# Attention and feed-forward kernel: the residual's mean and variance in the epilogue from sums that ScalarE accumulates, in place of VectorE's statistics

## The reference, cut to what matters

```
def _layernorm(x, axis=-1, eps=1e-05):
    m = jnp.mean(x, axis=axis, keepdims=True)
    v = jnp.var(x, axis=axis, keepdims=True)
    return (x - m) / jnp.sqrt(v + eps)
...
def _L0_ffn_ref(inputs, ln_w, ln_b, W1, b1, W2, b2):
    x = bf16_round(inputs)
    residual = bf16_round(inputs)
    h = mx_layernorm(x, ln_w, ln_b)      # mean and variance of the bf16 residual
    h = mx_linear(h, W1, b1)             # mx_quant of h and W1, 512 -> 2048
    h = mx_gelu(h)
    h = mx_linear(h, W2, b2)             # 2048 -> 512
    return bf16_round(residual + h)
...
    x = x + _L0_xattn_ref(_layernorm(x), ctx_2048, ...)
    x = x + _L0_ffn_ref(_layernorm(x), ...)
```

## Time and profile before

| | |
|---|---|
| median of 3 runs | 2685.33 us (2680.43 to 2685.69) |
| profiled execution: time | 2687.95 us |
| profiled execution: span | 2686.2 us |
| granted TensorE clock, mean | 0.844 |
| busy: VectorE, TensorE, ScalarE, GpSimd | 92%, 82%, 75%, 54% |

### The profile page before, as it was taken

One profiled execution on the slowest core, in us unless ns is written; L12 is line 12 of the kernel. 1 busy time (PEld: TensorE's weight loads), 2 busy tenths in 40 slices (PEclk: granted clock), 3 DMA queues, 4 the chain that ended last, 5 costly groups with the idle time before them and its releaser, 6 DMA issues. The chain is left out here.

```text
span 2686.2 us, 53043 instructions
## 1 busy us (share of the span) xinstructions
PE 2212.1 (82%) x20020; PEld 1181.0 (44%) x20020; DVE 2478.9 (92%) x3614; ACT 2009.7 (75%) x1862; POOL 1443.9 (54%) x1879
## 2 busy tenths in 40 slices
PE   8999999788887787777888888787787777868886
PEld 4454445344444444444444444444444444433433
DVE  6998758699999999999999999999999999957997
ACT  4454444389888888888888888888888888855655
POOL 2432322155767666676666667676666767551001
PEclk9999999877778877887677777878878888779999
DMA  7566454699999999999999999999999999990000
GB/s 234 145 154 143 97 135 101 150 184 182 193 193 203 202 179 201 199 189 184 191 205 173 205 201 186 191 198 203 178 199 202 183 199 177 175 226 19 16 20 24
DMA packets 1406612, 445.65 MB, mean 166 GB/s; under 512 B 1337444, under 2 KB 1377892, under 8 KB 1405256
## 3 DMA queue, kind: packets, MB, share of 16 engines
q1 hardware_dynamic: 1391816, 403.47, 80.4%
q10 hardware_dynamic: 14624, 40.06, 5.9%
HBM read 80.66 MB, written 44.02 MB: 46 GB/s over the span
## 5 line engine op out<-in xcount | busy, mean ns | idle before, releaser
L913 DVE TENSOR_SCALAR_CACHE_REDUCE arena<-a_ps_s 128x1281 f32<-128x1281 f32 (+1 forms) x1280 | 1824.3, 1488 | 23.7 <-PE a_ps_s L853 16.6
L960 ACT ACTIVATE arena<-arena,a_bias,a_row_scale 128x3328 uint8<-128x3328 f32 (+1 forms) x512 | 1560.5, 3049 | 241.9 <-POOL a_bias L1019 241.3
L853 PE MATMUL a_ps_s<-arena,q_rep 96*128 96x512 bf16 (+2 forms) x3840 | 1201.6, 434 | 345.6 <-DVE arena L913 313.9
L853 PEld LDWEIGHTS a_ps_s<-arena,q_rep 96*128 (+1 forms) x3840 | 310.7, 108 | 782.8 <-DVE arena L913 456.5
L866 PEld LDWEIGHTS a_ps_o<-v_head,a_nT 128*128 128x128 f16 x13056 | 524.3, 102 | 263.6 <-issue 148.5
L866 PE MATMUL a_ps_o<-v_head,a_nT 128*128 128x32 f16 x13056 | 514.1, 182 | 28.9 <-POOL a_nT L1027 26.2
L1026 POOL CAST a_nT<-arena 128x1664 int16<-128x1664 uint8 x256 | 401.8, 1569 | 211.1 <-DMA arena<-arena 205.7
L1027 POOL CAST a_nT<-arena 128x1664 int16<-128x1664 uint8 x256 | 402.8, 1573 | 0.0
L1015 POOL TENSOR_SCALAR a_row_max<-a_row_max,a_part_max 128x1 f32<-128x1 f32 x256 | 92.1, 360 | 348.4 <-DVE arena L913 339.8
L376 POOL TENSOR_TENSOR p_rest<-p_kq,p_parts 128x512 f32<-128x512 f32 (+1 forms) x51 | 74.9, 1469 | 286.0 <-ACT p_parts L486 286.0
L406 PE MATMUL p_ps_k<-p_wkv,p_ctxT 128*128 128x512 f32 (+1 forms) x408 | 185.3, 597 | 0.0
(11 more groups left out here) (150 smaller groups left out, 1936.0 us busy)
## 6 DMA issues: line engine op xcount, KB each, us to landing
k_parts_transposed<-arena SPq DMA_DIRECT2D x25, 768.0 KB, 6.5
values<-arena SPq DMA_DIRECT2D x51, 256.0 KB, 6.5
p_ctx<-in_ctx_dram SPq DMA_DIRECT2D x25, 512.0 KB, 5.0
arena<-k_parts_transposed ACTq DMA_DIRECT2D x42, 240.1 KB, 4.2
arena<-in_L_ffn_W_dram SPq DMA_DIRECT2D x8, 1024.0 KB, 8.1
arena<-k_parts_transposed ACTq DMA_DIRECT2D x42, 160.1 KB, 3.7
a_late_v<-values ACTq DMA_DIRECT2D x21, 288.0 KB, 4.0
a_late_v<-values ACTq DMA_DIRECT2D x21, 256.0 KB, 3.7
```

The source lines that it names most:

```text
L853: last = nc.tensor.matmul(ps_s[:, b, n0:n0 + w], q, k_parts[0:3 * HD, slot, start[c] + n0:start[c] + n0 + w], start=True, stop=True)
L913: nc.vector.tensor_scalar(s_row[:, u, start[c]:start[c] + size[c]], ps_s[:, (u + c) % 2, 0:size[c]], 1.0, None, ALU.mult, ALU.max, accum_o ...
L960: nc.scalar.activation(out, s_row[:, u, keys_of_half[half]], ACT.Exp, scale=row_scale[:, u, 0:1], bias=bias[:, u:u + 1], accum_out=zsum[:, ...
```

## The change

The residual's statistics leave VectorE. ScalarE, right behind the two residuals, passes over each twice: a Copy and a Square, each with `accum_out`, which sums the output along the row into `sums`. The written tile itself, `left`, is scratch and is written by all four; so each waits for the one before. VectorE makes mean and variance of both tiles of the pair from the sums at the end of the step, in three instructions on 128x2: mean = sum / C, square = -mean * mean, var = sum of squares / C + square. What went at the end of each tile's half now stands once per pair, in front of `variance`.

```diff
--- before.py
+++ after.py
@@ -1097,6 +1097,7 @@
     w1T, w2T = view(F * C // P // 2, BF16), view(F * C // P // 2, BF16)
     parts = view((F + C) // 2, BF16)[0:BIAS_ROWS]
     gT = view(FC * P, BF16).rearrange("p (u j k) -> p u j k", u=2, k=P)
+    left = view(C // 2, BF16)
     pre = view(F, BF16).rearrange("p (u o) -> p u o", u=2)
     w1 = w1T.rearrange("p (j o) -> p j o", o=F)
     w2 = w2T.rearrange("p (j o) -> p j o", o=C)
@@ -1104,7 +1105,8 @@
 
     with Phase(nc, "f") as ph:
         aT = ph.sb("aT", [P, 2, CC, P])
-        stats = ph.sb("stats", [P, 4, 6])
+        stats = ph.sb("stats", [P, 2, 6])
+        sums, square = ph.sb("sums", [P, 2, 2, 2]), ph.sb("square", [P, 2])
         mv = ph.sb("mv", [P, 2, 4, 2])
         var_eps, root, rec, rstd, shift = (ph.sb(n, [P, 2, 4]) for n in ("var_eps", "root", "rec", "rstd", "shift"))
         eps, half = ph.sb("eps", [P, 4]), ph.sb("half", [P, 4])
@@ -1135,7 +1137,7 @@
         aT_ready, aT_copied, p_ready, x1_ready = (ph.sem(n) for n in ("aT_ready", "aT_copied", "p_ready", "x1_ready"))
         steps_sem, var_ready, root_ready, small_ready = (
             ph.sem(n) for n in ("vector_steps", "var_ready", "root_ready", "small_ready"))
-        resid_ready, h_ready = ph.sem("resid_ready"), ph.sem("h_ready")
+        resid_ready, sums_ready, h_ready = ph.sem("resid_ready"), ph.sem("sums_ready"), ph.sem("h_ready")
         hq_ready, hT_ready, hT_copied = ph.sem("hq_ready"), ph.sem("hT_ready"), ph.sem("hT_copied")
         up_ready, pre_ready, g_ready, gq_ready = (ph.sem(n) for n in ("up_ready", "pre_ready", "g_ready", "gq_ready"))
         gT_ready, gT_copied, y_ready, y_taken = (ph.sem(n) for n in ("gT_ready", "gT_copied", "y_ready", "y_taken"))
@@ -1286,6 +1288,17 @@
                 nc.scalar.activation(resid[:, k, :], x1[:, k, :], ACT.Identity, scale=rstd[:, i, s:s + 1],
                                      bias=shift[:, i, s:s + 1]).then_inc(resid_ready, 1)
 
+            def sums_of_residual(k):
+
+                if k is None:
+                    return
+                i, s = k // 2 % 2, k % 2
+                act.wait_ge(resid_ready, k + 1)
+                for n, function in enumerate((ACT.Copy, ACT.Square)):
+                    after_first(act, sums_ready, 2 * k + n)
+                    nc.scalar.activation(left, resid[:, k, :], function,
+                                         accum_out=sums[:, i, n, s:s + 1]).then_inc(sums_ready, 1)
+
             def copy_hidden(k):
                 if k is None:
                     return
@@ -1330,6 +1343,8 @@
                 take(g_tiles[1])
                 for s in range(2):
                     residual(r_tiles[s])
+                for s in range(2):
+                    sums_of_residual(r_tiles[s])
                 copy_heads(x_tiles[1])
                 copy_gated(g_tiles[0])
                 take_output(g_tiles[0])
@@ -1403,13 +1418,17 @@
                 nc.vector.bn_aggr(mv[:, k // 2 % 2, k % 2, :], stats[:, k % 2, :]).then_inc(steps_sem, 1)
                 steps.value += 1
 
-            def moments_of_residual(k):
-                if k is None:
-                    return
-                dve.wait_ge(resid_ready, k + 1)
-                steps.then_wait(nc.vector.bn_stats(stats[:, 2 + k % 2, :], resid[:, k, :]))
-                nc.vector.bn_aggr(mv[:, (k // 2 + 1) % 2, 2 + k % 2, :], stats[:, 2 + k % 2, :]).then_inc(steps_sem, 1)
-                steps.value += 1
+            def moments_of_residuals(first):
+
+                if first is None:
+                    return
+                pair = first // 2
+                mean, var = (mv[:, (pair + 1) % 2, 2:4, n] for n in range(2))
+                dve.wait_ge(sums_ready, 4 * (pair + 1))
+                steps.then_wait(nc.vector.tensor_scalar(mean, sums[:, pair % 2, 0, :], 1.0 / C, None, ALU.mult))
+                steps.then_wait(nc.vector.scalar_tensor_tensor(square[:], mean, -1.0, mean, ALU.mult, ALU.mult))
+                steps.then_wait(nc.vector.scalar_tensor_tensor(var, sums[:, pair % 2, 1, :], 1.0 / C, square[:],
+                                                               ALU.mult, ALU.add))
 
             def variance(i):
                 dve.wait_ge(steps_sem, steps.value)
@@ -1445,7 +1464,7 @@
                     quantise_hidden(h_tiles[s])
                     round_output(2 * n - 1 + s)
                     add_projection(x_tiles[s])
-                    moments_of_residual(r_tiles[s])
+                moments_of_residuals(r_tiles[0])
                 if n + LEAD <= PAIRS:
                     variance(n + LEAD)
             round_output(NT - 1)
```

## The result

The changed kernel takes 2706.94 us (median of 4 runs, 2704.84 to 2713.83) against 2683.45 (2680.43 to 2685.69) for the kernel before on the same chip: ratio 1.0087, 95% interval [1.0072, 1.0102]. Slower by 23.5 us, by the interval 19.3 to 27.4; 2713 was forecast, with 2699 to 2722 as the range.

A forecast was written before the change was run, and what follows sets the result against it. The epilogue was bound by two equally long rings, VectorE's (30.85 us) and TensorE-ScalarE's (30.82), the second lengthened by the sums. Waits and edges +19 us plus clock +9 made +28, so 2713 us, range 2699 to 2722.

The forecast's parts named there:

- two rings: Epilogue dependency loops per two-tile step: VectorE's own, 30.85 us, and one through TensorE and ScalarE, 30.82 us.
- the middle case: ScalarE's four activations, each waiting for the previous accumulator read: 0.75 us apiece, 3.0 a pair, between 2.5 and 3.4.
- n = -2 and -1: Early epilogue steps (numbered -3 to 7): sums before the heads' copy cost +2.8 us in the first, +0 in the second.
- n = 0, wait: Epilogue step 0: sums delay the gated copy, which had 0.30 us of idle before it: +2.7 us.
- n = 1 to 4, waits: Four middle epilogue steps: no ScalarE idle before the gated copy, so 3.0 us each, +12.0 us.
- n = 5, wait: Last epilogue step with sums: 1.09 us of idle before the copy absorbs part of the cost: +1.9 us.
- n = 6, 7: Final epilogue steps, without sums: VectorE had a little slack against the root, about -0.4 us.
- clock: TensorE matmuls slow behind longer idle: 1.9 us each in steps 1 to 4, 0.7 each in 0 and 5, +9.0 us.
- The signs named in advance: Epilogue profile: VectorE idle 3 to 6 us, TensorE idle about 4.5, clock under 1.00, longer steps, activations 3.0 us.

The follow-up runs named there:

- e2: Changed kernel without ScalarE's four sums, VectorE making mean and variance from constants: 2686.25 us, ratio 1.0006 to the kernel before.
- e6: Kernel before with only the two residuals moved, each behind the copy of its gated tile: 2684.44 us, ratio 1.0007 to the kernel before.
- e5: e3 with each residual also moved into ScalarE's wait, right ahead of its sums: 2682.0 us, ratio 1.0000 to the kernel before.
- e1: Changed kernel with VectorE's bn_stats and bn_aggr back, ScalarE's sums made but not read: 2708.62 us, ratio 1.0088 to the kernel before.
- e3: Changed kernel with each tile's sums moved behind its gated copy, where ScalarE waits for TensorE: 2685.84 us, ratio 1.0011 to the kernel before.
- e7: Changed kernel with each of the four sum activations run twice, eight per pair: 2735.52 us, ratio 1.0204 to the kernel before.
- e4: Changed kernel with 16 extra bias matmuls filling TensorE's gap before the even down: 2705.73 us, ratio 1.0088 to the kernel before.
- e8: e5 with the plain sum taken from the residual's own activation, leaving one Square per tile: 2677.16 us, ratio 0.9970 to the kernel before.

## Why the prediction was right

**The bound.** Right: two rings of equal length, 30.85 and 30.82, of which the change shortens one and lengthens the other. e2, e6 and e5 show each. The 92% of VectorE was no evidence for a gain.

**Where the added work stands.** Right: it counts in full because of its place between the residuals and the gated copy (e1: all of the loss; e3: the same work elsewhere, none in the middle steps; e7: twice the work, a gap longer by 3.02 us more).

**Its size.** 3.0 us a pair was taken, 2.93 measured. Copy and Square take 0.61 to 0.63 us with 0.19 for the read, 0.74 from one start to the next for the same tile (2516.88 - 2516.14), the value of the middle case. The Trainium skill's figures (ScalarE: Activation LUTs, What ACT_TABLE_LOAD costs) would have given an estimate of 2.1 with every overlap kept. This trace doesn't agree: the second activation starts 0.03 us behind the end of the first one's read (2516.66 + 0.19 = 2516.85), and the trace decides.

**The sum, term by term.** The first two rows are from the changed kernel's trace, the waits behind them from e4, where the clock doesn't fall; "measured" adds up to the epilogue's +29.1.

| term | forecast, us | measured, us |
|---|---|---|
| n = -2 and -1 | +2.8 | -0.2 |
| n = 0, wait | +2.7 | +2.8 |
| n = 1 to 4, waits | +12.0 | +11.5 |
| n = 5, wait | +1.9 | +2.5 |
| n = 6, 7 | -0.4 | +0.2 |
| clock | +9.0 | +12.3 |

The waits of n = 0 to 5 are right, each row within 0.6 us. The first row (3.0 too much) and the clock (3.3 too little) are not, and they cancel. That the sum came out within about 1 us of the forecast's 28 is therefore luck in part.

**The clock's part.** For n = 1 to 4 it was right: the steps are 1.5, 2.6, 1.5 and 1.9 us longer than e4's, 7.5 in all, where 7.6 had been taken. The mis-sized terms are n = 0 and n = 5, with 0.7 each because their gaps are shorter. In n = 0 `ps_y` took 6.21 us behind 3.26 of idle, against 3.63; in n = 5 it took 5.6 behind 3.23, against 3.94 before. Against e4, the step behind the `down` of n = 0 is 2.6 us longer and the stretch from the `down` of n = 5 to the end 2.2.

**The start.** For n = -2 the forecast was +2.8, and the step from the first variance to the second went from 16.52 to 16.26 us. ScalarE's sums did stand in the way (2401.19 to 2404.13). But the prediction took the time from the first variance to the residuals as it stood in one trace, and it was not fixed. In the trace before, four of VectorE's small instructions on that path ran slowly beside GpSimd:

```profile
2411.90 1.19 DVE L1427 TENSOR_TENSOR f_rec<-f_rec,f_root 128x4 f32<-128x4 f32 x1
```

The four took 0.76, 1.19, 1.19 and 0.97 us while GpSimd added biases (2410.58 for 4.92 us), and the residuals began 5.58 us behind the variance. In the changed kernel's trace the same four took 0.16 each, the residuals began 2.13 behind it, and the copy of the heads 6.49 instead of 7.01 us behind it, in spite of 2.93 us of sums. The matmuls behind the heads then took 3.70 us behind 3.63 of idle, where they had taken 6.32 behind 4.15. GpSimd had waited 4.70 us for the transfer of `x` before these additions, so their place depends on when that arrives, and no experiment holds that fixed.

**The total.** +28 forecast; +29.1 in the epilogue of the two traces, +23.5 between the medians, with an interval (19.3 to 27.4) that does not reach 28. The attention's scatter of up to 15 us between traces is large enough for the difference, with four runs a side; that it makes it up was not shown.

**The signs named in advance** stood: idle in front of the first reciprocal 3.81 us (3 to 6 forecast), idle in front of `down` 4.67 (4.5), a clock under 1.00, steps of 35.3 and 36.4 (35 to 36), and 2.93 us (3.0) for the activations. Two did not. VectorE's second wait, for the projection, was not named. And the stages ahead of the epilogue, which "should not move at all", end 12.3 us earlier in this trace (first variance); the change does not touch them.

## What to carry to other kernels

Before moving work from the busiest engine to an idler one, look at what the receiving engine does at that place in its queue: an engine that is idle a third of the time can be on the critical ring just there, and a few places later the same work is free. Where two rings are equally long, shortening one shows no gain and is no proof that it was useless; change both (e2, e6, e5), and look at the first and last steps too: what e5 won in the middle it gave back there, and only e8 was faster as a whole. And a new gap in front of matmuls can be paid twice: once as the gap, and once as matmuls at a lower clock behind it, here 16.8 and 12.3 us by the table above.

## What had not been expected of the hardware

**Small VectorE instructions beside GpSimd.** In step -2 of the changed kernel the same three instructions that take 0.14 to 0.16 us elsewhere take eight times as long:

```profile
2410.12 1.23 DVE L1428 TENSOR_SCALAR f_mv<-f_sums 128x2 f32<-128x2 f32 x1
2411.39 1.18 DVE L1429 SCALAR_TENSOR_TENSOR f_square<-f_mv 128x2 f32<-128x2 f32 x1
2412.60 1.20 DVE L1430 SCALAR_TENSOR_TENSOR f_mv<-f_sums,f_square 128x2 f32<-128x2 f32 x1
2413.90 1.12 DVE L1435 TENSOR_TENSOR f_var_eps<-f_mv,f_eps 128x4 f32<-128x4 f32 x1
```

GpSimd is adding biases at that time, eight instructions of 128x512 in a row:

```profile
2407.60 9.83 POOL L1181 TENSOR_TENSOR arena<-arena,vectors 128x512 f32<-128x512 f32 x8 [2.94 <-DMA arena<-in_x_dram]
```

9.83 / 8 = 1.23 us is the length of one of them, so each small instruction seems to wait for one to end; the reciprocals in the same stretch take 0.18 us as always. From the first of the four to the end of the variance it is 4.9 us instead of 0.8.

The ten traces agree. From 2380 us on they hold 618 such instructions on 128x2 and 128x4 (tensor_scalar, scalar_tensor_tensor and tensor_tensor). Of these, 548 ran beside no GpSimd instruction, and none took over 0.17 us; 70 overlapped one, and 61 took over 0.5 us. All 180 reciprocals took 0.18 us, 16 of them beside GpSimd. No experiment moved GpSimd's work, so the cause is inferred from this coincidence. It also explains a row of the prediction: the mean of 252 ns for L1430 is that of eight instructions of 0.16 us and one of 0.97 beside GpSimd, and no price of the instruction by itself.

**The clock's price alternates.** In steps of almost equal length, `ps_y` behind the same 4.67 us of idle took 5.12, 6.25, 5.14 and 6.26 us in turn. In e1 the same series came again, 5.18, 6.28, 5.15, 6.26; in e7, with steps of 38.5 and 39.7, 5.39, 6.58, 5.51, 4.95. Other places show the same: eight matmuls of the projection behind 3.63 or 3.64 us of idle took 3.70 us in the changed kernel and in e1, 5.40 in e4 and 6.45 in e3. The granted clock says how the time differs (0.70 over the 5.12 us, 0.57 over the 6.25), so the low level lasted for a shorter or longer part of the same matmuls; what sets that stays open.
